# Axis stages of a four-layer network: the first tile's front released before the decay matrix is built, the building shared by three engines, the weights loaded by two queues

## The reference

```
def selective_scan(u, delta, A, B, C, D):
    A = clip(A, -5, 5)
    dA = einsum('bld,dn->bldn', delta, A)
    dB_u = einsum('bld,bld,bln->bldn', delta, u, B)
    c = flip(cumsum(flip(concat(dA[:, 1:], 0))))      # sums over later positions
    c = exp(min(c, 15))
    x = cumsum(dB_u * c, axis=1) / (c + 1e-6)
    return einsum('bldn,bln->bld', x, C) + u * D
def mamba(x, ...):
    x1, res = split(x @ in_w.T)
    x1 = silu(causal_conv4(x1) + conv_b)
    A = -exp(clip(A_log, -5, 5))                      # 192 x 96
    x_dbl = x1 @ xproj_w.T
    delta = softplus(x_dbl[..., :6] @ dproj_w.T + dproj_b)
    y = selective_scan(x1, delta, A, B, C, Dp)
    return y * silu(res) @ out_w.T
# h_out = bn(mamba along h), w_out = bn(mamba along w), layer 1 = h_out + w_out + x
```

## Time and profile before

| | us |
|---|---|
| median of 3 runs | 19240.01 (19239.32 to 19246.41) |
| profiled execution | 19243.72 |
| its span | 19241.8 |
| busy: DVE / PE / POOL / ACT | 17802.0 / 16257.4 / 15292.2 / 13962.1 |
| height stage, from its first weight issue | 1624.75 |
| width stage, from its first weight issue | 9488.64 |

### The profile page before, as it was taken

How to read it: one execution, slowest core, us unless ns; L and a number is a source line. 1 busy time by engine, 2 the same in 40 slices (tenths; PEclk the granted TensorE clock), 3 DMA queues, 4 the chain that set the end, 5 groups by cost and what they waited for, 6 DMA issues and landing times. The chain is left out here.

```text
span 19241.8 us, 290646 instructions
## 1 busy us (share of the span) xinstructions
PE 16257.4 (84%) x60328; PEld 8303.8 (43%) x60424; DVE 17802.0 (93%) x48666; ACT 13962.1 (73%) x18390; POOL 15292.2 (79%) x10500
## 2 busy tenths in 40 slices
PE   5776888888888888888688888888888888887777
PEld 2223444444444444444344444444444444442222
DVE  4998999999999999999899999999999999984888
ACT  4665777777777777777577777777777777761666
POOL 1554999889888998888699999999999999970444
PEclk8998999999999999999899999999999999996999
DMA  1000000000000000000000000000000000000000
GB/s 33 13 13 12 11 11 11 11 11 11 11 11 11 11 11 11 11 11 11 12 11 11 11 11 11 11 11 11 11 11 11 11 11 11 11 10 20 10 12 11
DMA packets 778173, 227.53 MB, mean 12 GB/s; under 512 B 747760, under 2 KB 750476, under 8 KB 776332
## 3 DMA queue, kind: packets, MB, share of 16 engines
q1 hardware_dynamic: 776332, 206.79, 8.2%
HBM read 143.66 MB, written 62.97 MB: 11 GB/s over the span
## 5 line engine op out<-in xcount | busy, mean ns | idle before, releaser
L1222 POOL TENSOR_TENSOR h_sm<-h_sm,h_wr 128x768 f32<-128x768 f32 x2944 | 5400.3, 1834 | 755.2 <-DVE h_wr L1002 669.6
L1222 POOL TENSOR_TENSOR w_sm<-w_sm,w_wr 128x768 f32<-128x768 f32 x2944 | 5399.1, 1834 | 502.5 <-DVE w_wr L1002 404.6
L1386 PE MATMUL w_pz<-w_xr,w_tri 128*128 128x384 f32 x9984 | 4462.6, 530 | 788.2 <-DVE w_wr L1002 622.5
L1386 PE MATMUL h_pz<-h_xr,h_tri 128*128 128x384 f32 x9984 | 4424.7, 526 | 770.6 <-DVE h_wr L1002 604.5
L1002 DVE SCALAR_TENSOR_TENSOR h_wr<-h_pz,h_bct,h_rbuf 128x192 f32<-128x192 f32 x11776 | 4250.3, 407 | 171.9 <-PE h_pz L1386 171.2
L1002 DVE SCALAR_TENSOR_TENSOR w_wr<-w_pz,w_bct,w_rbuf 128x192 f32<-128x192 f32 x11776 | 4243.4, 408 | 96.1 <-PE w_pz L1386 95.5
L976 DVE SCALAR_TENSOR_TENSOR w_xr<-w_cbuf,w_bct,w_pdx 128x192 f32<-128x192 f32 x9984 | 3634.9, 405 | 76.0 <-issue 35.2
L976 DVE SCALAR_TENSOR_TENSOR h_xr<-h_cbuf,h_bct,h_pdx 128x192 f32<-128x192 f32 x9984 | 3632.6, 404 | 75.7 <-issue 35.2
L1098 ACT ACTIVATE h_cbuf<-h_pe_e,h_consts 128x1024 f32<-128x1024 f32 x2304 | 2526.1, 1112 | 1532.4 <-PE h_pe_e L1374 1332.1
L1098 ACT ACTIVATE w_cbuf<-w_pe_e,w_consts 128x1024 f32<-128x1024 f32 x2304 | 2526.1, 1112 | 1492.7 <-PE w_pe_e L1374 1305.1
L604 POOL TENSOR_TENSOR m_gv<-m_hs,m_cv 128x512 f32<-128x512 f32 x1024 | 1351.0, 1322 | 2240.9 <-DVE m_hs L468 2213.4
(11 more groups left out here) (355 smaller groups left out, 19595.9 us busy)
## 6 DMA issues: line engine op xcount, KB each, us to landing
h_lt<-pieces_s SPq DMA_DIRECT2D x512, 96.0 KB, 4.4
w_lt<-pieces_s SPq DMA_DIRECT2D x512, 96.0 KB, 4.3
pieces_s<-h_pieces SPq DMA_DIRECT2D x384, 48.0 KB, 2.1
pieces_s<-w_pieces SPq DMA_DIRECT2D x384, 48.0 KB, 2.1
h_xt<-first_s SPq DMA_DIRECT2D x34, 128.0 KB, 5.5
w_xt<-first_s SPq DMA_DIRECT2D x34, 128.0 KB, 3.1
m_u<-hn_s SPq DMA_DIRECT2D x32, 128.8 KB, 2.7
m_u<-slots_s SPq DMA_DIRECT2D x32, 128.8 KB, 2.6
```

Source lines behind the costliest of these rows:

```text
L1222: tt(sm[:, g], sm[:, g], wr[:, u % 3], ALU.add).then_inc(s_add, 1)
L1386: t.matmul(pz[:, P % 2, 0:2 * DX], tri[:], x, start=True, stop=True).then_inc(s_z, 1)
```

## The change

In `phase_axis`, which runs twice:

1. The transfers of weights are issued by two engines. SyncE keeps 15 of the 27 (ident, the eight of A_log, cols, bn, rows); ScalarE issues 12 (inT, upT, dtT, taps, down, outw, xpr, xpT). All still count on `s_w`.
2. The tile `xt` is cleared first, with a semaphore `s_pad`; SyncE waits for that one, and not for `s_go`, ahead of the load of the first input.
3. The first clip of A moves ahead of the other preparation and has its own semaphore `s_clip`.
4. The six memsets that raise `s_go` come ahead of the second clip and the pieces of A (now `a_pieces`), which VectorE does right after them, ahead of `make_xc` of tile 0.
5. The 16 instructions that spread `asel` into `decay` are shared: VectorE makes 3 between `make_xc` and `prefix` and 4 after `prefix`; GpSimd makes 3 after `piece3`; ScalarE makes 6 after `sig_z`. TensorE waits for the three shares (`s_dec`) ahead of the first fill. ScalarE waits for `asel` ahead of `piece1`, since `around` lies in `pieces`.

The diff, cut to its core:

```
@@ sync
                 ld(ident[:], ident_in)
-                ld(inT, w["inT"])
-                ld(upT, w["upT"])
...
+                sp.wait_ge(s_pad, 1)
+                load_x(place(0), 0)
                 sp.wait_ge(s_go, 1)
-                load_x(place(0), 0)
@@ vector
-                for big in (inw, inz, wdt, wbc, wo, xt):
+                v.memset(xt[:], 0.0).then_inc(s_pad, 1)
+                for big in (inw, inz, wdt, wbc, wo):
...
                 dve.wait_ge(s_w, 16 * NW)
+                v.tensor_scalar(am, am, -5.0, 5.0, ALU.max, ALU.min).then_inc(s_clip, 1)
...
-                v.tensor_scalar(am, am, -5.0, 5.0, ALU.max, ALU.min).then_inc(s_aexp, 1)
-                dve.wait_ge(s_aexp, 3)
-                step(v.tensor_scalar(am, am, 5.0, None, ALU.min))
...
-                for d in range(16):
-                    last = v.tensor_scalar(decay[:, :, :, d], asel.rearrange("p (m n) -> p m n", n=NX), low4[:, d:d + 1],
-                                           None, ALU.mult)
-                step(last)
                 for m, (s, n) in enumerate([(s_r, 2), (s_wd, 2), (s_add, UN), (s_res, 1), (s_e, 2 * GRP), (s_go, 1)]):
                     v.memset(mark[:, m:m + 1], 0.0).then_inc(s, n)
+
+                def a_pieces():
+                    dve.wait_ge(s_aexp, 2)
+                    step(v.tensor_scalar(am, am, 5.0, None, ALU.min))
...
+                    v.scalar_tensor_tensor(asel, around, pick[:, 2:3], asel, ALU.mult, ALU.add).then_inc(s_asel, 1)
+                    dve.wait_ge(s_asel, 1)
+
+                def make_decay(d):
+                    return v.tensor_scalar(decay[:, :, :, d], asel.rearrange("p (m n) -> p m n", n=NX),
+                                           low4[:, d:d + 1], None, ALU.mult)
...
+                a_pieces()
                 make_xc(0, 0)
+                for d in range(3):
+                    make_decay(d)
                 prefix(0)
+                for d in range(3, 7):
+                    last = make_decay(d)
+                last.then_inc(s_dec, 1)
                 make_gate(0, 0)
@@ scalar
+                def ld(dst, src):
+                    act.dma_start(dst, src).then_inc(s_w, 16)
+                ld(inT, w["inT"])
+                ld(upT, w["upT"])
...
-                act.wait_ge(s_aexp, 2)
+                act.wait_ge(s_clip, 1)
                 a.activation(am, am, ACT.Exp).then_inc(s_aexp, 1)
...
+                act.wait_ge(s_asel, 1)
                 piece1(0)
                 piece2(0)
                 sig_z(3)
+                for d in range(10, 16):
+                    last = a.activation(decay[:, :, :, d], asel.rearrange("p (m n) -> p m n", n=NX), ACT.Identity,
+                                        scale=low4[:, d:d + 1])
+                last.then_inc(s_dec, 1)
@@ gpsimd
                 piece3(0)
+                for d in range(7, 10):
+                    last = nc.gpsimd.tensor_scalar(decay[:, :, :, d], asel.rearrange("p (m n) -> p m n", n=NX),
+                                                   low4[:, d:d + 1], None, ALU.mult)
+                last.then_inc(s_dec, 1)
@@ tensor
                 pe.wait_ge(s_lt[0], 128)
+                pe.wait_ge(s_dec, 3)
```

More of the change, by code:

```diff
@@ L753, in phase_axis @@
         s_go, s_xt, s_pd = sem(tag + "prepared"), sem(tag + "input"), sem(tag + "pieces_stored")
+        s_pad, s_clip, s_asel, s_dec = (sem(tag + n) for n in ("input_cleared", "a_clipped", "a_pieces", "decay_made"))
         s_lt = [sem(tag + "pieces_loaded0"), sem(tag + "pieces_loaded1")]
@@ L926, in _ @@
                 step(v.tensor_tensor(bsc[:, 1:2], bn[:, 1:2], bsc[:, 2:3], ALU.subtract))
-                v.tensor_scalar(am, am, -5.0, 5.0, ALU.max, ALU.min).then_inc(s_aexp, 1)
-                dve.wait_ge(s_aexp, 3)
-                step(v.tensor_scalar(am, am, 5.0, None, ALU.min))
[L931 to L938, removed]
-                for d in range(16):
-                    last = v.tensor_scalar(decay[:, :, :, d], asel.rearrange("p (m n) -> p m n", n=NX), low4[:, d:d + 1],
-                                           None, ALU.mult)
-                step(last)
                 for m, (s, n) in enumerate([(s_r, 2), (s_wd, 2), (s_add, UN), (s_res, 1), (s_e, 2 * GRP), (s_go, 1)]):
                     v.memset(mark[:, m:m + 1], 0.0).then_inc(s, n)
+                def a_pieces():
+                    dve.wait_ge(s_aexp, 2)
+                    step(v.tensor_scalar(am, am, 5.0, None, ALU.min))
+                    step(v.tensor_copy(around, am))
+                    v.tensor_scalar(asel, around, pick[:, 0:1], None, ALU.mult)
+                    step(v.tensor_tensor(arest, am, around, ALU.subtract))
+                    step(v.tensor_copy(around, arest))
+                    v.scalar_tensor_tensor(asel, around, pick[:, 1:2], asel, ALU.mult, ALU.add)
+                    step(v.tensor_tensor(arest, arest, around, ALU.subtract))
+                    step(v.tensor_copy(around, arest))
+                    v.scalar_tensor_tensor(asel, around, pick[:, 2:3], asel, ALU.mult, ALU.add).then_inc(s_asel, 1)
[3 more added lines that the diff above has]
+                                           low4[:, d:d + 1], None, ALU.mult)
                 def make_xc(F, q):
@@ L1038, in _ @@
                 a = nc.scalar
+                def ld(dst, src):
+                    act.dma_start(dst, src).then_inc(s_w, 16)
+                ld(inT, w["inT"])
+                ld(upT, w["upT"])
+                ld(dtT, w["dtT"])
+                ld(taps, w["taps"].rearrange("k (j d) -> k j d", j=JB).partition_broadcast(128))
+                for g in range(2):
+                    q = slice(64 * g, 64 * g + 64)
+                    ld(down2[:, q], w["down"])
+                    ld(outw2[:, :, g, :], w["outw"].rearrange("e (j d) -> e j d", j=JB))
+                    ld(xpr2[:, :, g, :], w["xpr"].rearrange("r (j d) -> r j d", j=JB))
+                    ld(xpT[q], w["xpT"].rearrange("(j d) n -> d j n", j=JB))
                 act.wait_ge(s_prep, 1)
```

6 lines of the change are left out of this document (removed).

## The result

The changed kernel took 19173.33 us (median of 7 runs, 19161.70 to 19191.94), the kernel before, beside it, 19243.58 us (7 runs, 19236.25 to 19258.15): a ratio of 0.9964 [0.9953, 0.9976]. It is 70 us faster, where 110 were forecast, and 19173 lies outside the range of 19112 to 19156. The profiled execution took 19161.7 us, its span 19159.9, at a granted TensorE clock of 0.96 in both kernels; its two stage starts show nearly the whole difference.

What follows compares the result with a forecast made beforehand. VectorE, busy 93% of the span, was the bound; the change touches only the two axis-stage starts. Height 56.8 plus width 53.6 saves 110.4 us of 19243.7, giving 19133.3, predicted as 19130; range 19112 to 19156.

Steps and rivals of the forecast that it cites:

- Weights: Stage start, first issue to weights in: 11.0 us instead of 16.06, near the transfers' bound, saving 5.1 us a stage.
- the loading isn't shortened: Rival: ScalarE's issues or the shared 16 engines eat the loading gain, 5.1 us a stage back, 19140; chance 0.10.
- Preparation to the release: Stage start, weights in to the release: 11.85 us; saved 55.5 (height) and 55.7 (width), weights included.
- release to `xc`: Stage start: `xc` 9.5 us after the release, behind VectorE's pieces of A, instead of 14.52 and 11.12; saved 5.0 and 1.6.
- Contention: After the scan: VectorE's spreading and GpSimd's instructions take turns, delaying the last piece by 3.7 us a stage.
- no exclusion: Rival: VectorE's spreading and GpSimd do not block each other, so 3.7 us a stage comes back, 19122; chance 0.20.
- four in a row let nobody in: Rival: VectorE keeps its place, delay 9.9 us a stage instead of 3.7, 19142; chance 0.25, shared with a late share.
- The shares: Spreading before the first fill: ScalarE 2.4 us apiece, ending 32.8 after `xc`; GpSimd at most 3.0, ending 33.0; both hidden.
- a share is late: Rival: GpSimd's share at 5 us apiece, 12 us more in all, 19142; chance 0.25, shared with VectorE keeping its place.
- The fill: First fill starts 33.3 us after `xc` (29.6 before plus 3.7), waiting for `lt` and not for a share.

Runs made afterwards that it cites:

- e4_loads: The kernel before with only the twelve weight issues moved to ScalarE's queue; 19227.74 us, against 19253.82 for the kernel before beside it.
- e8_wait_pc: The changed kernel with VectorE's four spreading instructions behind the scan held until GpSimd has made the last piece of `sfx`; 19163.51 us in one run.
- e6_tt_wait: The changed kernel with `decay` made by twelve contiguous VectorE instructions, the eight behind the scan waiting for GpSimd's last piece; 19131.21 us, ratio 0.9937.
- e2_no_act: The changed kernel without ScalarE's six spreading instructions; GpSimd clears `decay` at the stage start instead; 19160.60 us in one run.
- e5_tt: The changed kernel with `decay` made by twelve contiguous VectorE instructions, four before the scan and eight after, without a wait; 19147.12 us, ratio 0.9946.
- e1_step1: The changed kernel with all 16 spreading instructions writing contiguous blocks instead of every sixteenth element; 19122.84 us, against 19253.82 for the kernel before.
- e9_step2: The changed kernel with the 16 spreading instructions writing one element in 2 (4 bytes); 19156.26 us, against 19256.71 for the kernel before.
- e10_step8: The changed kernel with the 16 spreading instructions writing one element in 8 (16 bytes); 19163.78 us, against 19256.71 for the kernel before.
- e7_after_again: The changed kernel as it is, timed again beside the versions with twelve VectorE instructions; 19173.62 us (median of 5), ratio 0.9959 to the kernel before.

## Why the prediction was wrong

*Weights.* Forecast 11.0 us, measured 12.34 and 12.55. The bound was the right one, the transfers', and 8.8 us of transfers with 1.5 of ending would be 10.3; e4_loads, without the input beside them, came to 11.2 and 11.7. The input's transfers beside ScalarE's loads were left out of the sum, and may be the rest. The miss is 2.9 us of the missing 34.9. The input itself was hidden, as forecast. The Trainium skill (DMA: Bandwidth & Descriptors, section "Issuing engines are not separate DMA queues") calls the gain of a second issuer usually small; here 15.0 us of issuing stood over 8.8 of transfer, and e4_loads saved 4.9 and 4.2 us. The rival "the loading isn't shortened" falls.

*Preparation to the release; release to `xc`.* 11.85 forecast, 11.8 measured; 9.5 forecast, 9.43 measured, in nearly every kernel, with no idle time ahead of `xc`. Right. But the pieces of A cost only 0.3 us more than the convolution hides, not 1.0: the other chain, to the end of `sig_x` at 1652.32, took 9.1 us and not 8.5, since TensorE's bias at the release takes 1.64 us (from 1643.30), and the forecast had used the shorter one behind `xc`, 1.03.

*Contention.* The mechanism was right: VectorE's spreading instruction and GpSimd's instructions exclude each other, in turns. e8_wait_pc and e6_tt_wait show it from both sides. The rival "no exclusion" falls, and so does the one in which four in a row let nobody in (9.9). The size was 5.6 us at the last piece instead of 3.7, since each of the three instructions met a spreading one, `sfx` and the remainder and the last piece, not two of them. The Trainium skill (SBUF — State Buffer, section "Who interferes with whom") has the shared port pair, held for a whole instruction; the 0.82 of `sfx` alone against 3.17 beside VectorE agrees, and ScalarE's unchanged 29.4 us too.

*The shares: the step that failed.* The prediction took 2.4 us apiece for ScalarE, "stepped writes cost it 603 - 468 = 135 ns for 128 elements", and 3.0 for GpSimd, "at most 3.0 for 1152 if the spread write costs it nothing". Measured are 4.9 and 7.3. ScalarE's start was 1.4 us later than the 18.6 forecast (20.0), its six took 29.5 instead of 14.2: they ended at 49.5 instead of 32.8, and the fill came at 49.6 instead of 33.3. Over both stages that is 32.5 of the missing 34.9 us; the loading is the rest, less half a microsecond in the other steps. GpSimd's share, ending at 42.8, was late as well, hidden behind ScalarE's (e2_no_act). The rival "a share is late" had named GpSimd at 5 us and 12 us in all for the two stages; the late engine was ScalarE, and the lateness nearly three times that.

What was wrong in the reading: the earlier trace rows gave a surcharge of 1.05 ns an element from two groups with different destinations, at 128 elements, and it was scaled to 1152. Both groups write float32, the stepped one at 264 bytes from element to element (`acc` has rows of 66), and read `pf`, TensorE's output; the spreading reads `asel` and writes bfloat16. Which of these differences makes the surcharge three times as large, no run shows. The measured surcharge is 3.2 ns an element (4.9 less 1.2, over 1152). And VectorE's own rows, 2.48 stepped against 0.76 contiguous, had shown a factor of 3.3 for this very destination. ScalarE's came to 4.2 times (29.49 against 6.97) and GpSimd's to 2.3. The row of the same destination on another engine was the nearer one, and it would have given 3.8 us for ScalarE and 9.9 for GpSimd, both late. The bound was named ("at VectorE's price with overhead, 2.75, they would be 1.8 late"), with an absolute price where the ratio was the thing to carry over. The range inherited this: it held ScalarE at 2.75 at worst.

The Trainium skill (SBUF — State Buffer, section "Door 1: The DMA port swizzle", its note on "cachelines") has lines of 16 bytes, of which one must be hit at least twice in succession for the full rate. The runs agree: a step of 4 bytes hits four elements in 16 bytes and costs 0.04 to 0.3 us, one of 16 bytes hits one and costs as much as one of 32. The same note lets bfloat16 stride 8 elements for free; at 8 elements, 16 bytes, the runs show the full cost, and they decide. By the rule the forecast could have asked how much is lost, not whether; the runs gave the amount.

*The fill.* What would have come without the shares is seen in e5_tt: with the last piece at 18.5, the fill at 32.7, 14.3 behind it, as in the kernel before. The chain of store and load was forecast rightly, and so were the bodies, which kept their lengths within 2 us.

What stays open: how much of the loading the early input costs, for which there are too few runs without it, and why TensorE's clock was lower in some stage starts. The single runs lie up to 22 us off what their stage starts say against the kernel before (255.1): 131.0 against 111.9 in e1_step1, 100.5 against 111.7 in e9_step2, 92.9 against 71.3 in e10_step8, 26.1 against 10.1 in e4_loads. That is the unchanged rest, which differs by 33 us between profiles. In the seven runs of the changed kernel the longer ones have the lower granted clock over the whole span (19162 us at 0.963, 19173 to 19179 at 0.962, 19192 at 0.961), in the five of e7_after_again only roughly so; that the clock is the cause isn't shown.

## What to carry to other kernels

Price an instruction that is moved to another engine by its destination pattern, not by its element count: take the ratio of stepped to contiguous from the same destination, and where none is in the trace, keep the bound at several times the contiguous price. Before work is shared, look whether its form is what makes it dear: twelve contiguous instructions on one engine cost 20 us, sixteen stepped ones 40 on that engine, and split over three engines they cost 21 us of VectorE's time and 51 of the others'. Work that is to be hidden behind a chain on GpSimd must not run on VectorE while that chain does; one wait was worth some 6.5 us over two stages.

## What the runs showed of the hardware

The cost of a stepped bf16 write by distance between elements, in us for 128x1152 from f32 (ScalarE and GpSimd: total over count, VectorE: the minimum, undisturbed by GpSimd; GpSimd's 7.5 and 7.3 hold one wait for VectorE, without it they are 7.1 and 7.0):

| distance | ScalarE | GpSimd | VectorE |
|---|---|---|---|
| 2 bytes | 1.2 | 3.2 | 0.81 |
| 4 bytes | 1.4 | 3.5 | 0.85 |
| 16 bytes | 5.2 | 7.5 | 2.78 |
| 32 bytes | 4.9 | 7.3 | 2.76 |

Some 2 to 4 us are added on every engine, all between 4 and 16 bytes; what 8 bytes cost wasn't tried.

A long instruction of GpSimd can hold one of VectorE up until it ends. In e2_no_act it cleared the buffer from 1622.82 to 1638.28; VectorE's clip, ready at 1634.30, is recorded with 4.58 us instead of 0.76 and ends 0.6 behind it. VectorE's memsets ran beside it at their usual lengths.

```profile
1629.40 0.06 DVE L886 MEMSET h_mask<- 128x6 f32 x1
1634.30 4.58 DVE L888 TENSOR_SCALAR h_rbuf<-h_rbuf 128x1152 f32<-128x1152 f32 x1 [4.83 <-DMA h_brow<-in_H_rows]
```

That put the release of this kernel 15.6 and 15.2 us behind the weights, instead of 11.8.
